# First attention: products, maxima and turned row of its first group made among the feed-forward products of the first layer

## The chip, the cores and the metric

The kernel runs on one core of a Trainium2 chip. The core has a matrix engine (TensorE, "PE" in the rows, its weight loads "PEld"), a vector engine (VectorE, "DVE"), a scalar engine (ScalarE, "ACT"), GpSimd ("POOL") and a queue that issues most transfers (SyncE, "SP" or "SPq"). They run side by side and wait for each other through semaphores. The metric is the device time of one execution in microseconds (us), lower is better; of several runs the median is given.

## The reference

Two transformer layers on x of 2 x 1024 x 256 in float32. The change lies in the first layer, where the feed-forward part and an attention of 16 heads of width 16 read the same normalised input `xn`:

```python
x = x + _L0_attn_ref(xn, ...) + _L0_ffn_ref(xn, ...)

# feed-forward: 256 -> 768 -> 256
fuse = silu(qmm(x, gate_w, gate_scale)) * qmm(x, up_w, up_scale)
return qmm(fuse, down_w, down_scale)

# attention: the plain scores, and the same with a "splat" term added
std_out = out_proj(softmax(where(mask, scores, neg)))
gsa_scores = scores + position_sensitivity * splat_attn
gsa_out = out_proj(softmax(where(mask, gsa_scores, neg)))
return (1.0 - blend) * std_out + blend * gsa_out
```

The second layer (a memory attention with sorting, a second attention, and a mixture of experts) is not touched.

## The kernel before, in words

The kernel is a list of stages. In each, every engine runs its own function (`pe`, `act`, `dve`, `pool`, `sp`), and all wait at the end of a stage until the others are there (`stage_end`). Three stages matter.

**Queries and keys** computes the records of queries and keys and stores them in the chip's main memory; its stores may go on into the next stage.

**AttentionStart together with SwiGLU** is the feed-forward part. The 2048 rows of x go in 4 blocks of 512, the 768 hidden columns in 6 slices of 128. A step is one block and one slice: 24 steps, numbered (block, slice) from (0, 0). TensorE makes in a step the four gate products `pg` and the four up products `pu`; from the second block on, slices 1 to 4 also carry the 12 down products `py` of a quarter of the block before. ScalarE makes silu (`sg`) and a rounded copy (`fh`). VectorE makes `fz` (fusing gate and up, L650), `fl` (the rest of the rounding, one step late, L656) and, in slices 2 to 5, `y` (scaling of `py`, L669). GpSimd adds `y` to x (L677). After the 24th step the down products of the last block remain. Within each engine this order is written out by hand. `pg`, `pu` and `py` have two buffers each in the accumulator memory (PSUM).
In the same stage `AttentionStart.clear` lets GpSimd wait for the stores of the records and then clear two of three places for queries and keys (L777, L778); `AttentionStart.sp` then loads groups 0 and 1 of the attention into them (16 transfers each, L761). `clear` is called by `SwiGLU.pool` after its fourth addition.

**Attention** works in 16 groups of two heads, each with plain and splat scores. A group needs, before its first score, a row that holds the negative maximum of every query. For it TensorE makes 20 units of products (`px`, L973 for the mask and L979), VectorE takes the negative maxima of each unit out of `px` (`negmax`, L1063, 20 reductions of 512 to 1024 elements on each partition), combines them (L1067, L1071), TensorE turns the result (L986), VectorE copies it (`rows`, L1078), and SyncE sends it into the queries' place (L937). `px` has two buffers. The scores (`pss`, L998) then follow, ScalarE takes the exponential (`probs`, L1035), and TensorE multiplies with the values (`po`, L1012). The order of all this is a string (`ORDERS`) in which s is a score, m a unit of maxima, v a product with values, r the row, d and t the end of a half. The m and the r of a pass through the string belong to the next group: while group g is scored, the maxima of group g + 1 are made. `schedule` puts the 20 units and the row of group 0 ahead of the first pass, since no pass precedes it.

Of the kernel before, what the change touches and what calls it, by code (L numbers as in the profile page):

```python
# [16 lines left out]
P = 128  # L17
# [553 lines left out]
class SwiGLU(Stage):  # L571
# [5 lines left out]
    SLOTS = FC + 3  # L577

    def __init__(self, k, w, start):
# [10 lines left out]
        self.gate_in, self.up_in, self.silu_made, self.fused, self.fh_made, self.fl_made, self.down_in, self.scaled, self.added = k.sems(  # L590
            "gate_in up_in silu_made fused fh_made fl_made down_in scaled added")

    def pe(self, e):
        w = self.w
        e.wait_ge(w.scales_loaded, 48)
        for i in range(NB + 1):
            x = slice(i * 512, i * 512 + 512)
            for f in range(FC):
                b, m = f % 2, i * FC + f
                if i < NB:  # L600
                    if m >= 2:
                        e.wait_ge(self.silu_made, m - 1)
                    products(e, self.pg[b][:], [(w.gw[:, c, f * P:(f + 1) * P], a[:, c, x]) for c in range(DC)
                                                for a in (self.xh, self.xl)]).then_inc(self.gate_in, 1)
                    if m >= 2:
                        e.wait_ge(self.fused, m - 1)
                    products(e, self.pu[b][:], [(w.uw[:, c, f * P:(f + 1) * P], a[:, c, x]) for c in range(DC)
                                                for a in (self.xh, self.xl)]).then_inc(self.up_in, 1)
                if i and 1 <= f <= 4:
                    n = 4 * (i - 1) + f - 1  # L610
                    e.wait_ge(self.fl_made, i * FC)
                    if n >= 2:
                        e.wait_ge(self.scaled, n - 1)
                    ts = slice((f - 1) * P, f * P)
                    products(e, self.py[n % 2][:], [(part[self.slot(i - 1, g)][:, ts], w.dw[:, g, :]) for g in range(FC)
                                                    for part in (self.fh, self.fl)]).then_inc(self.down_in, 1)

# [22 lines left out]
    def dve(self, e):  # L640
        k, w = self.k, self.w
        for m in range(NB * FC + 1):
            if m < NB * FC:
                f, b = m % FC, m % 2
                e.wait_ge(self.silu_made, m + 1)
                e.wait_ge(self.up_in, m + 1)
                if m >= 3:
# [3 lines left out]
                                       ALU.mult, ALU.mult).then_inc(self.fused, 1)  # L651
            if m:
# [18 lines left out]
    def pool(self, e):  # L671
        k = self.k
        for n in range(NT):
            if n == 4:
# [112 lines left out]

class AttentionTiles:
# [15 lines left out]
class Attention(Stage):  # L804
# [19 lines left out]
    def __init__(self, k, operands, t, records):  # L824
        self.k, self.ops, self.t, self.records = k, operands, t, records
        self.order = self.ORDERS[operands.nk]
# [96 lines left out]
    def sp(self, e):  # L923
        k, tl, t = self.k, self.ops, self.t
        for what, g, _, _ in self.units:
# [8 lines left out]
            elif what == "rows":  # L934
                e.wait_ge(self.x_read, self.places(g, "rows", None))
                rows = f32(tl.qs[g % 3][STACK:STACK + HALF + 1:HALF, :, :]).rearrange("r w (t q) -> r (w t) q", t=QT)
                e.dma_start(rows, f32(t.rows[g % 2][:])).then_inc(self.row_sent, 16)  # L937
        for p in range(3):
            e.wait_ge(self.loaded[p], 16 * tl.PARTS * len(range(p, tl.groups, 3)))
        e.wait_ge(self.row_sent, 16 * tl.groups)  # L940
# [6 lines left out]
    def pe(self, e):  # L947
        k, tl, ops = self.k, self.t, self.ops
        places, scores, maxed, std_place = 0, 0, -1, {}
        for what, g, w, arg in self.units:  # L950
# [4 lines left out]
            if what == "max":  # L955
                width, parts = arg
                diag = [t * P + P == c + width for t, c in parts][0]
# [5 lines left out]
                fresh = not ops.adds(w)  # L963
                if fresh:
# [3 lines left out]
                if diag and fresh:  # L968
                    for side in range(2):
                        for n in range(2):  # L970
                            at = HALF * n
                            to = px[:, n, 0:len(parts) * width].rearrange("p (s k) -> p s k", k=width)
                            e.matmul(to[:, :, width - P + HALF * side:width - HALF + HALF * side],  # L973
                                     k.mask_of[at:at + HALF, side, :], k.mask_by[at:at + HALF, side, 0:len(parts), :],
                                     start=side == 0, stop=False, skip_group_check=True)
                for s, (t, c) in enumerate(parts):
                    for n in range(2):
                        _, tile, at, _ = ops.of[w + n]
                        x = e.matmul(px[:, n, s * width:(s + 1) * width], ops.qs[p][at:at + STACK, tile, t * P:(t + 1) * P],  # L979
                                     ops.ks[p][at:at + STACK, tile, c:c + width], start=fresh and not diag, stop=True,  # L980
                                     skip_group_check=True)
                x.then_inc(self.x_in, 1)
            elif what == "rows":
                e.wait_ge(self.max_whole, g + 1)
                e.wait_ge(self.x_read, places - 1)
                e.matmul(px[0:4 * QT, 0, 0:P], tl.negmax[g % 2][:, 0].rearrange("p w t -> p (w t)"), k.ident[:],  # L986
                         start=True, stop=True).then_inc(self.x_in, 1)
            elif what == "scores":
# [4 lines left out]
                if scores % 48 == 0:  # L993
                    e.wait_ge(self.row_sent, 16 * (g + 1))
# [49 lines left out]
    def dve(self, e):  # L1044
        tl = self.t
        places, turns, rec, most_steps = 0, 0, Steps(self.rec_steps), Steps(self.max_steps)
        for what, g, w, arg in self.units:
# [3 lines left out]
            if what == "max":  # L1051
                width, parts = arg
                a, b = self.ops.place(w), self.ops.place(w + 1)
                of = slice(a, b + 1, b - a) if b > a else slice(a, None if b == 0 else b - 1, b - a)
                e.wait_ge(self.x_in, places)
                if len(parts) == 2:
                    out = tl.negmax[g % 2][:, :, of, parts[0][0]]
                    from_px = px[:, :, 0:2 * width].rearrange("p n (s k) -> p s n k", s=2)
                else:
                    (t, c), = parts  # L1060
# [1600 lines left out]
```

## Time and profile before

| | us |
|---|---|
| median of 3 runs | 1931.88 (1930.86 to 1935.39) |
| the profiled execution | 1928.34 |
| its span, from the first to the last instruction | 1926.6 |
| TensorE busy | 1698.7 (88%) |
| VectorE busy | 1484.1 (77%) |
| ScalarE busy | 1236.1 (64%) |
| GpSimd busy | 709.5 (37%) |

The span is what the profile sees; the time of the execution has 1.74 us around it. In the rows below all starts are in us from the start of the span. The feed-forward stage runs from 130.0 to about 203, the first attention from 203.2 on.

### The profile page before, as it was taken

The numbers are of one execution on the slowest core, as the hardware profiler recorded it, in microseconds if no ns is written. First come the engines' busy times: TensorE is split into PE (matmuls) and PEld (weight loads), VectorE is DVE, ScalarE is ACT, GpSimd is POOL, SyncE is SP. The second block draws the span as 40 slices with busy tenths as digits, with TensorE's granted clock in tenths as the row PEclk, the third lists the DMA queues.
The fourth block names the chain that finished last, engine by engine and source line by source line (L and its number), as shares of the span: only waits on it lengthen the run. The fifth ranks groups of instructions, "written<-read, shape, count | busy, mean of one in ns | idle before, by whom it ended". The sixth has DMA issues, their size and how long they took to land. (4 is left out here: it accounts for less than half of the span.)

```text
span 1926.6 us, 32116 instructions
## 1 busy us (share of the span) xinstructions
PE 1698.7 (88%) x10626; PEld 1186.8 (62%) x10626; DVE 1484.1 (77%) x3097; ACT 1236.1 (64%) x2770; POOL 709.5 (37%) x1334
## 2 busy tenths in 40 slices
PE   3989799999999888788789998887977899987998
PEld 3558444444444467576668876766865455545887
DVE  6765789999997258999997879999357698826654
ACT  2544278887778534788886678888542488865322
POOL 2003212122222215666675556666143111224632
PEclk9999599999999889888989998899988699987999
DMA  3373122333430200000000000000036333110001
GB/s 120 125 225 67 34 52 55 62 67 67 68 67 3 74 1 1 1 1 1 1 1 1 1 1 1 1 1 1 1 103 178 48 61 68 35 59 15 1 1 45
DMA packets 36132, 82.53 MB, mean 43 GB/s; under 512 B 9600, under 2 KB 11776, under 8 KB 34944
## 3 DMA queue, kind: packets, MB, share of 16 engines
q1 hardware_dynamic: 35968, 80.48, 17.2%
q8 instruction: 86, 1.41, 0.3%
q14 instruction: 78, 0.64, 0.1%
HBM read 52.79 MB, written 27.26 MB: 42 GB/s over the span
## 5 line engine op out<-in xcount | busy, mean ns | idle before, releaser
L1035 ACT ACTIVATE probs<-pss 128x512 f32<-128x512 f32 (+3 forms) x1152 | 481.7, 496 | 128.3 <-PE pss L998 127.2
L1063 DVE TENSOR_REDUCE negmax<-px 128x2 f32<-128x1024 f32 (+2 forms) x480 | 507.2, 1113 | 43.0 <-PE px L979 39.9
L1602 POOL TENSOR_SCALAR rp<-sw,tau 128x256 f32<-128x256 f32 x720 | 341.3, 507 | 7.1
L1112 POOL TENSOR_SCALAR_AFFINE_SELECT probs<-probs 128x512 f32<-128x512 f32 x192 | 120.4, 635 | 534.4 <-ACT probs L1035 534.4
L998 PE MATMUL pss<-queries,keys 64*128 64x512 f32 (+3 forms) x1152 | 295.8, 396 | 10.3 <-ACT probs L1035 5.2
L979 PE MATMUL px<-keys,queries 63*128 63x512 f32 (+3 forms) x1152 | 271.7, 429 | 13.3 <-DVE negmax L1063 13.2
L998 PEld LDWEIGHTS pss<-queries,keys 64*128 64x128 f32 x1152 | 167.4, 191 | 157.4 <-ACT probs L1035 135.7
L1012 PE MATMUL po<-probs,vals 128*32 128x512 f32 (+3 forms) x2304 | 248.8, 508 | 0.4 <-POOL probs L1112 0.2
L1451 PE MATMUL pss<-again,sw 128*128 128x256 f32 x1024 | 243.9, 397 | 0.0
L1756 DVE BATCH_NORM_STATS2 st<-rp 128x6 f32<-128x512 f32 x360 | 229.6, 674 | 2.3 <-POOL rp L1602 2.3
L1451 PEld LDWEIGHTS pss<-again,sw 128*128 128x128 f32 x1024 | 202.8, 202 | 28.5
L1436 PE MATMUL pt<-ident,sw 128*128 128x128 f32 x768 | 133.9, 306 | 83.2 <-ACT sw L1536 47.9
L1506 ACT ACTIVATE ra<-sw,neg 128x256 f32<-128x256 f32 x432 | 183.6, 525 | 4.0 <-DVE neg L1669 4.0
L979 PEld LDWEIGHTS px<-keys,queries 63*128 63x128 f32 x1152 | 133.7, 202 | 70.1 <-DVE negmax L1063 65.7
L1536 ACT ACTIVATE sw<-sw,neg 128x256 f32<-128x256 f32 x384 | 165.8, 502 | 11.8 <-DVE neg L1732 11.8
L1436 PEld LDWEIGHTS pt<-ident,sw 128*128 128x128 f32 x768 | 98.1, 155 | 120.9 <-ACT sw L1536 94.0
L1766 DVE MAX8 top<-sw 128x8 f32<-128x256 f32 x384 | 148.9, 406 | 12.6 <-ACT sw L1530 12.6
L1530 ACT ACTIVATE sw<-pss 128x1024 f32<-128x1024 f32 x96 | 97.0, 1018 | 69.1 <-PE pss L1451 48.6
L1752 DVE BATCH_NORM_STATS2 st<-ra 128x6 f32<-128x512 f32 x216 | 137.8, 671 | 3.5 <-ACT ra L1506 2.8
L1522 ACT ACTIVATE sw<-pt 128x512 f32<-128x512 f32 x192 | 108.5, 590 | 27.4 <-PE pt L1436 27.2
L1460 PE MATMUL pz<-to_out,sw 128*128 128x256 f32 x512 | 122.8, 384 | 0.0
L1451 PE MATMUL pss<-vals,xt 128*128 128x256 f32 x512 | 119.6, 394 | 1.8 <-ACT sw L1530 1.6
(366 smaller groups left out, 2645.0 us busy)
## 6 DMA issues: line engine op xcount, KB each, us to landing
queries<-rec_q SPq DMA_DIRECT2D x96, 128.0 KB, 3.6
keys<-rec_k SPq DMA_DIRECT2D x96, 128.0 KB, 3.8
queries<-rec_q SPq DMA_DIRECT2D x96, 64.0 KB, 3.5
keys<-rec_k SPq DMA_DIRECT2D x96, 64.0 KB, 3.6
rec_q<-fs SPq DMA_DIRECT2D x16, 256.0 KB, 4.1
rec_k<-fs SPq DMA_DIRECT2D x16, 256.0 KB, 4.7
rec_q<-vals SPq DMA_DIRECT2D x16, 256.0 KB
rec_k<-vals SPq DMA_DIRECT2D x16, 256.0 KB
```

What stands on the lines that cost most here:

```text
L979: x = e.matmul(px[:, n, s * width:(s + 1) * width], ops.qs[p][at:at + STACK, tile, t * P:(t + 1) * P], ops.ks[p][at:at + STACK, tile, c:c ...
L998: e.matmul(tl.pss[scores % 3][:, 512 - width:512], ops.ks[p][at:at + STACK + 1, tile, j * P:(j + 1) * P], ops.qs[p][at:at + STACK + 1, til ...
L1012: x = e.matmul(tl.po[32 * n:32 * n + 32, 512 - width:512], self.vals[:, u // H * QT + j, u % H, :], tl.probs[arg][:, n, :], start=j == 0, ...
L1035: e.activation(tl.probs[arg][:, w, :], tl.pss[scores % 3][:, 512 - width:512], ACT.Exp).then_inc(self.exp_made, 1)
L1063: e.tensor_reduce(out, from_px, X_AXIS, ALU.max, negate=True).then_inc(self.x_read, 1)
L1436: x = e.transpose(self.pt[n % 2][:, 2 * h + c, :], self.view(g, q)[:, h, c * P:(c + 1) * P], k.ident[:])
L1451: x = e.matmul(self.pss[n % 2][:, h, :], lhsT, rhs[:, 4 * half + h, c, :], start=c == 0, stop=c == 1)
L1506: x = e.activation(self.ra[n % 7][:, :, h], self.view(g, q)[:, h, :], ACT.Relu, bias=self.negated(g, r)[:, 2 * q + h:2 * q + h + 1])
L1536: x = e.activation(self.view(g, q)[:, h, :], self.view(g, q)[:, h, :], ACT.Relu, bias=self.negated(g, 3)[:, 2 * q + h:2 * q + h + 1])
L1602: x = e.tensor_scalar(self.rp[rp % 6][:, :, h], self.view(g, q)[:, h, :], -BIG, self.tau[r][:, 2 * q + h:2 * q + h + 1], ALU.min, ALU.max)
L1756: e.bn_stats(st[:, q, :], self.rp[self.bn_p % 6][:].rearrange("p n h -> p (n h)")).then_inc(self.rp_read, 1)
L1766: e.max(self.top[g % 4][:, 8 * i + h, :], self.sw[g % 5][:, i, h, :]).then_inc(self.top_made, 1)
```

## The change

The 20 units, the combination, the turn, the copy and the transfer of the row of group 0 leave the attention stage and go into the feed-forward stage, into a class of their own (`FirstMaxima`). A table `MAXIMA` says in which steps of the third and fourth block how many units are made: two in slices 1 to 4, one in slice 5 and in slice 0 of the next block. In a step with two, TensorE makes the first between `pg` and `pu`, the second at the end of the step; VectorE takes the first maximum ahead of `fz`, the second behind it. They have one `px` of their own, of two banks, so each product waits until the maximum before it has been read. The turn stands behind the down products of (4, 1), and VectorE's combining and copying between the last `fl` and the last four `y`. SyncE sends the row behind the loads. `AttentionStart.clear` is now called ahead of GpSimd's first addition. In the attention stage, `schedule` starts with the first pass for group 0, whose first score waits for the transfer of the row (`sent`).

```diff
 class SwiGLU(Stage):
     SLOTS = FC + 3
+    MAXIMA = {(2, 1): 2, (2, 2): 2, (2, 3): 2, (2, 4): 2, (2, 5): 1, (3, 0): 1, (3, 1): 2, (3, 2): 2, (3, 3): 2,
+              (3, 4): 2, (3, 5): 1, (4, 0): 1}
...
             self.py = [k.ps("py", [P, D]) for _ in range(2)]
+            first.px = k.ps("px", [P, 2, 512])
...
+                extra = iter(self.maxima(i, f))
                 if i < NB:
...
                     products(e, self.pg[b][:], ...).then_inc(self.gate_in, 1)
+                    for n in islice(extra, 1):
+                        self.first.product(e, n)
...
                     products(e, self.pu[b][:], ...).then_inc(self.up_in, 1)
                 if i and 1 <= f <= 4:
...
+                for n in extra:
+                    self.first.product(e, n)
+                if (i, f) == (NB, 1):
+                    self.first.turn(e)
...
     def dve(self, e):
+            extra = iter(self.maxima(m // FC, m % FC))
             if m < NB * FC:
+                for n in islice(extra, 1):
+                    self.first.largest(e, n)
...
                 e.scalar_tensor_tensor(self.fz[m % 3][:], ...).then_inc(self.fused, 1)
+            for n in extra:
+                self.first.largest(e, n)
             if m:
...
+        self.first.row(e)
+        self.first.copy(e)
         for n in range(4 * (NB - 1), 4 * NB):
             self.scale(e, n)
...
     def pool(self, e):
         for n in range(NT):
-            if n == 4:
+            if n == 0:
                 self.start.clear(e)
...
+class FirstMaxima:
+    def product(self, e, n):
+        if n:
+            e.wait_ge(self.x_read, n)
+        else:
+            e.wait_ge(self.ops.loaded[0], 16 * self.ops.PARTS)
+        maximum_products(e, self.k, self.ops, 0, *self.units[n], self.px).then_inc(self.x_in, 1)
+    def largest(self, e, n):
+        e.wait_ge(self.x_in, n + 1)
+        largest_of(e, self.ops, *self.units[n], self.px, self.negmax).then_inc(self.x_read, 1)
...
 class Attention(Stage):
     def schedule(self):
-        yield from self.maxima(0)
-        yield "rows", 0, None, None
+        if self.begun is None:
+            yield from self.maxima(0)
+            yield "rows", 0, None, None
...
                 if scores % 48 == 0:
-                    e.wait_ge(self.row_sent, 16 * (g + 1))
+                    if g or self.begun is None:
+                        e.wait_ge(self.row_sent, 16 * (g + 1 - self.before))
+                    else:
+                        e.wait_ge(self.begun.sent, 16)
```

`maximum_products` and `largest_of` hold what stood in `Attention.pe` and `Attention.dve` before.

VectorE in the fourth block, slices 3 and 4 (steps of the feed-forward stage). Before:

```order
L669 TENSOR_TENSOR y<-py,dsc 128x256
L650 SCALAR_TENSOR_TENSOR fz<-pu,us,sg 128x512
L656 TENSOR_TENSOR fl<-fz,fh 128x512
L669 TENSOR_TENSOR y<-py,dsc 128x256
L650 SCALAR_TENSOR_TENSOR fz<-pu,us,sg 128x512
L656 TENSOR_TENSOR fl<-fz,fh 128x512
```

Now the same two steps:

```order
L695 TENSOR_TENSOR y<-py,dsc 128x256
L848 TENSOR_REDUCE negmax<-px 128x2
L672 SCALAR_TENSOR_TENSOR fz<-pu,us,sg 128x512
L848 TENSOR_REDUCE negmax<-px 128x2
L680 TENSOR_TENSOR fl<-fz,fh 128x512
L695 TENSOR_TENSOR y<-py,dsc 128x256
L848 TENSOR_REDUCE negmax<-px 128x2
L672 SCALAR_TENSOR_TENSOR fz<-pu,us,sg 128x512
L848 TENSOR_REDUCE negmax<-px 128x2
L680 TENSOR_TENSOR fl<-fz,fh 128x512
```

Each step got two reductions, one on either side of `fz`, where there were three instructions there are five.

TensorE from the last down products of the feed-forward stage into the attention. Before, the 20 units of group 0 (`px`, L973 and L979) follow:

```order
L137 MATMUL py<-dw,fl 128x256
L973 MATMUL px<-mask_by,mask_of 128x2x64 x4
L979 MATMUL px<-keys,queries 128x128 x4
L973 MATMUL px<-mask_by,mask_of 128x2x64 x4
L979 MATMUL px<-keys,queries 128x256 x4
L979 MATMUL px<-keys,queries 128x128 x4
L979 MATMUL px<-keys,queries 128x256 x4
L973 MATMUL px<-mask_by,mask_of 128x64 x4
```

and behind their last products stand the turn, the first two units of group 1 and only then the first scores (`pss`):

```order
L973 MATMUL px<-mask_by,mask_of 128x64 x4
L979 MATMUL px<-keys,queries 128x512 x22
L986 MATMUL px<-ident,negmax 32x128
L973 MATMUL px<-mask_by,mask_of 128x2x64 x4
L979 MATMUL px<-keys,queries 128x128 x4
L973 MATMUL px<-mask_by,mask_of 128x2x64 x4
L979 MATMUL px<-keys,queries 128x256 x4
L998 MATMUL pss<-queries,keys 128x512 x2
L979 MATMUL px<-keys,queries 128x128 x4
```

Now the last down products are followed at once by group 1's first units and the scores of group 0:

```order
L137 MATMUL py<-dw,fl 128x256
L824 MATMUL px<-mask_by,mask_of 128x2x64 x4
L830 MATMUL px<-keys,queries 128x128 x4
L824 MATMUL px<-mask_by,mask_of 128x2x64 x4
L830 MATMUL px<-keys,queries 128x256 x4
L1103 MATMUL pss<-queries,keys 128x512 x2
L830 MATMUL px<-keys,queries 128x128 x4
L1103 MATMUL pss<-queries,keys 128x384
```

GpSimd ahead of and in the feed-forward stage. Before:

```order
L310 MEMSET vals 128x8192
L312 MEMSET vals 128x256
L677 TENSOR_TENSOR x<-x,y 128x256 x4
L777 MEMSET queries 128x2048
L778 MEMSET keys 128x2048
L777 MEMSET queries 128x2048
L778 MEMSET keys 128x2048
L677 TENSOR_TENSOR x<-x,y 128x256 x12
```

Now all four clearings of the places stand ahead of the sixteen additions:

```order
L310 MEMSET vals 128x8192
L312 MEMSET vals 128x256
L803 MEMSET queries 128x2048
L804 MEMSET keys 128x2048
L803 MEMSET queries 128x2048
L804 MEMSET keys 128x2048
L703 TENSOR_TENSOR x<-x,y 128x256 x16
```

## Rows read from the trace of the kernel before

**Rows 1.** Windows: us, busy and (instructions) of each engine, clock, DMA share, GB/s

```profile
205.00:210.00 5.00, 3.48 (x24) 1.95 (x22) 4.70 (x6) 0.00 (x0) 1.81 (x2) 0.50 0.00 0
...
230.00:235.00 5.00, 4.15 (x27) 3.36 (x25) 3.33 (x4) 4.92 (x10) 0.64 (x1) 0.50 0.95 181
...
240.00:245.00 5.00, 5.00 (x36) 1.77 (x36) 3.59 (x5) 2.98 (x7) 0.00 (x0) 0.79 0.00 0
```

**Rows 2.** Timeline, opening of the attention: start, us, engine, line, out<-in, [idle before <-releaser]

```profile
203.21 0.29 PE L973 MATMUL px<-mask_by,mask_of 64*128 64x128 bf16 x4 [1.39 <-POOLq L2549]
...
203.84 2.42 DVE L1063 TENSOR_REDUCE negmax<-px 128x4 f32<-128x512 f32 x3 [1.55 <-PE px L979]
...
206.56 18.56 DVE L1063 TENSOR_REDUCE negmax<-px 128x4 f32<-128x1024 f32 x17 [0.30 <-PE px L979]
...
226.62 0.60 SPq L937 DMA_DIRECT2D queries<-rows  x1
...
227.02 2.00 DVE L1063 TENSOR_REDUCE negmax<-px 128x4 f32<-128x512 f32 x2 [0.48 <-PE px L979]
...
228.69 0.80 PE L998 MATMUL pss<-queries,keys 64*128 64x512 f32 x2 [0.94 <-DMA queries<-rows]
...
229.57 1.28 ACT L1035 ACT_TABLE_LOAD   x1 [35.78 <-PE pss L998]
...
229.85 0.69 DVE L1063 TENSOR_REDUCE negmax<-px 128x4 f32<-128x512 f32 x1 [0.83 <-PE px L979]
```

**Rows 3.** Timeline, the rows' transfers of groups 1 and 2, and a maximum between

```profile
254.42 0.55 SPq L937 DMA_DIRECT2D queries<-rows  x1
...
257.62 1.82 DVE L1063 TENSOR_REDUCE negmax<-px 128x4 f32<-128x512 f32 x2 [1.46 <-PE px L979]
...
280.32 0.51 SPq L937 DMA_DIRECT2D queries<-rows  x1
```

**Rows 4.** Timeline of VectorE, feed-forward stage, one light step

```profile
159.18 0.75 DVE L650 SCALAR_TENSOR_TENSOR fz<-pu,us,sg 128x512 f32<-128x512 f32 x1
159.84 0.68 DVE L656 TENSOR_TENSOR fl<-fz,fh 128x512 fp32r<-128x512 f32 x1
160.44 0.42 DVE L669 TENSOR_TENSOR y<-py,dsc 128x256 f32<-128x256 f32 x1
160.99 0.75 DVE L650 SCALAR_TENSOR_TENSOR fz<-pu,us,sg 128x512 f32<-128x512 f32 x1
```

**Rows 5.** Timeline of TensorE, feed-forward stage, one step with down products

```profile
187.03 0.40 PE L137 MATMUL pg<-xh,gw 128*128 128x512 f32 x1
...
188.87 0.28 PE L137 MATMUL py<-dw,fh 128*128 128x256 f32 x1
...
190.28 0.40 PE L137 MATMUL pg<-xh,gw 128*128 128x512 f32 x1
```

**Rows 6.** Timeline, a unit's pair of products at full clock, first attention

```profile
250.75 0.54 PE L979 MATMUL px<-keys,queries 63*128 63x512 f32 x2
```

**Rows 7.** Timeline, end of the feed-forward stage

```profile
194.71 0.58 PE L137 MATMUL py<-dw,fh 128*128 128x256 f32 x1 [2.43 <-DVE fl L656]
...
201.87 0.43 DVE L669 TENSOR_TENSOR y<-py,dsc 128x256 f32<-128x256 f32 x1 [0.94 <-PE py L137]
```

**Rows 8.** Timeline, GpSimd's first addition and clearing, SyncE's first load

```profile
151.26 0.73 POOL L677 TENSOR_TENSOR x<-x,y 128x256 f32<-128x256 f32 x1 [136.79 <-DVE y L669]
...
161.61 1.83 POOL L777 MEMSET queries<- 128x2048 f32 x1
...
165.28 0.82 SPq L761 DMA_DIRECT2D queries<-rec_q  x2
```

**Rows 9.** Windows: the end of the stores, and of the loads of both groups

```profile
144.00:146.00 2.00, 2.00 (x11) 1.62 (x10) 1.35 (x2) 1.39 (x4) 0.00 (x0) 1.00 0.05 19
184.00:186.00 2.00, 2.00 (x12) 1.70 (x11) 0.43 (x2) 1.10 (x2) 0.73 (x1) 1.00 0.19 23
```

**Rows 10.** Windows, TensorE busy for half of a stretch, memory attention

```profile
910.00:916.00 6.00, 3.22 (x16) 2.32 (x15) 6.00 (x18) 3.92 (x8) 1.52 (x5) 1.00 0.00 0
```

More of the change, by code:

```diff
@@ L591, in __init__, with maxima @@
             "gate_in up_in silu_made fused fh_made fl_made down_in scaled added")
+    def maxima(self, i, f):
+        at = sum(c for where, c in self.MAXIMA.items() if where < (i, f))
+        return range(at, at + self.MAXIMA.get((i, f), 0))
     def pe(self, e):
@@ L785, in sp, with maximum_products @@
             t.load(self.k, e, p)
+def maximum_products(e, k, ops, g, w, arg, px):
+    width, parts = arg
+    diag = [t * P + P == c + width for t, c in parts][0]
+    fresh = not ops.adds(w)
+    if diag and fresh:
+        for side in range(2):
+            for n in range(2):
+                at = HALF * n
+                to = px[:, n, 0:len(parts) * width].rearrange("p (s k) -> p s k", k=width)
+                e.matmul(to[:, :, width - P + HALF * side:width - HALF + HALF * side],
+                         k.mask_of[at:at + HALF, side, :], k.mask_by[at:at + HALF, side, 0:len(parts), :],
+                         start=side == 0, stop=False, skip_group_check=True)
+    for s, (t, c) in enumerate(parts):
+        for n in range(2):
+            _, tile, at, _ = ops.of[w + n]
+            x = e.matmul(px[:, n, s * width:(s + 1) * width], ops.qs[g % 3][at:at + STACK, tile, t * P:(t + 1) * P],
+                         ops.ks[g % 3][at:at + STACK, tile, c:c + width], start=fresh and not diag, stop=True,
+                         skip_group_check=True)
+    return x
@@ new lines, in largest_of @@
+def largest_of(e, ops, w, arg, px, negmax):
+    width, parts = arg
+    a, b = ops.place(w), ops.place(w + 1)
+    of = slice(a, b + 1, b - a) if b > a else slice(a, None if b == 0 else b - 1, b - a)
+    if len(parts) == 2:
+        out = negmax[:, :, of, parts[0][0]]
+        from_px = px[:, :, 0:2 * width].rearrange("p n (s k) -> p s n k", s=2)
+    else:
+        (t, c), = parts
+        out = negmax[:, c // 512, of, t % 4 if c else t]
+        from_px = px[:, :, 0:width]
+    return e.tensor_reduce(out, from_px, X_AXIS, ALU.max, negate=True)
@@ L962, in pe @@
                     e.wait_ge(self.x_read, places - 2)
-                fresh = not ops.adds(w)
-                if fresh:
+                if not ops.adds(w):
                     std_place[arg] = places
@@ L967, in pe @@
                     assert places == std_place[arg] + 2
[L968 to L982, printed above, removed]
+                maximum_products(e, k, ops, g, w, arg, px).then_inc(self.x_in, 1)
             elif what == "rows":
-                e.wait_ge(self.max_whole, g + 1)
-                e.wait_ge(self.x_read, places - 1)
+                e.wait_ge(self.max_whole, g + 1 - self.before)
+                if places > 1:
+                    e.wait_ge(self.x_read, places - 1)
                 e.matmul(px[0:4 * QT, 0, 0:P], tl.negmax[g % 2][:, 0].rearrange("p w t -> p (w t)"), k.ident[:],
@@ L2485, in stages @@
             k.blend = k.sb("blend", [P, 4, 4])
+            opening = FirstMaxima(k)
             with ExitStack() as held:
```

73 lines of the change are left out of this document (47 added, 26 removed).

## The prediction

> **What bounds the kernel now.** I began with the shares of busy time in the table of the profile: TensorE 88%, VectorE 77%. As a mean they would say that TensorE is the limit everywhere. The windows say otherwise for one place. In [rows 1], first row, which stands for the opening of the attention, VectorE is busy for 4.70 of 5 us, TensorE for 3.48 at half its clock (0.50 granted, 1.2 GHz), and ScalarE for nothing. So the 20 maxima of group 0 are a stretch in which VectorE alone sets the pace and nothing else of the kernel goes on. The timeline [rows 2] gives it in order. The stage starts at 203.21, the first maximum at 203.84, the 20 reductions take 2.42 + 18.56 = 20.98 us (1.09 each on the mean; one of 1024 elements about 1.13), the row is sent at 226.62, and the first score begins at 228.69, when the transfer has landed 2.07 us later. The reader is to see that every one of these waits for the one before.
>
> The feed-forward stage is the opposite. There the timeline of TensorE [rows 5] shows a step with down products from 187.03 to 190.28, 3.25 us without a gap: 1.84 for the eight gate and up products, 1.41 for the twelve down products. A light step takes 1.81 us (159.18 to 160.99 in [rows 4]). VectorE needs per step 0.66 for `fz`, 0.60 for `fl` and 0.55 for `y`, each from start to start in [rows 4]: 1.81 in all. In a step of 3.25 it thus has 1.44 us free.
>
> **What the change removes.** The stage will begin with the same products and reductions as before, but those of group 1. Group 1's first maximum began at 227.02; it will begin where group 0's did, 0.63 us into the stage. That is 227.02 - 203.84 = 23.2 us less, for everything behind it at an unchanged pace. The scores no longer wait for the transfer: TensorE idled 0.94 us for it, and VectorE 0.83 us for the product queued behind that score [rows 2]. I add 0.8 for this. What is late next is ScalarE's table load of 1.28 us, which comes with the first exponential as before. Bounds from the nearest rows: nothing more than the 23.2, or 4.7 us more, if the first pass ran like the second. It took 27.4 us from its first maximum to the transfer of its row (227.02 to 254.42), the second 22.7 (257.62 to 280.32) [rows 2, 3]. The difference is that the first ran at half clock until about 241 ([rows 1], 0.50 and then 0.79), and had the table load. I take 24.0, with 23.2 and 27.9 as ends, since the stage still opens with light work on TensorE.
>
> **What it adds to the feed-forward stage.** First VectorE's work alone. At 160.99 it starts `fz` of step (2, 0) and is free, `fl` included, at 162.25, about when the first product can be there. From then to the last `fl` it has 11 `fz` (7.3), 12 `fl` (7.2), 8 `y` (4.4) and the 20 maxima (21.0): 39.8 us, so it ends at 202.1. Before, TensorE resumed behind the last `fl` at 194.71 [rows 7]. Without any wait the stretch is thus 7.4 us longer. This is the lower end, and it shows where the gain goes: 1.44 us free per step don't hold two maxima of 1.13.
>
> Then the waits between the two. TensorE needs little: a pair of products of 512 columns takes 0.54 from start to end [rows 6], and since such a pair overlaps, I count 0.3 of issue. But there is one `px`. In a step with two units: from the end of a second product, its maximum is read 1.25 us later (handover and 1.13), and only then the next step's first product can go; the four gate products (0.92) are over by then. After it come 0.3 + 0.92 + 1.41 + 0.3 = 2.93 for itself, up, down and the second product, and some 0.15 for the handover. The ring closes in 4.3 us, against 4.07 of VectorE's own work (1.81 + 2 x 1.13). So a step goes from 3.25 to 4.3. Eight such steps give 8.4; the first six units are narrower, and two of them, the 512-element ones, take half, which brings this to 7.4. The four steps with one unit: VectorE had no time free where there is a `y`, so (2, 5) and (3, 5) each grow by 1.13, and so does (4, 0), where the maximum stands ahead of the last `fl`; (3, 0) has no `y` and grows by 0.6. Together 4.0. The turn and the copy stand ahead of the last `y`s, and TensorE's third group of down products waits for the first of these; I give 0.3. The sum is 11.7 us. It is the same as 7.4 without waits, plus 0.2 of wait for each of 20 maxima, plus 0.3. For that wait the ends are 0 and 0.83, the longest that VectorE waited for such a product in [rows 2]: 7.7 and 24.3 us in all. I stay at 0.2, since other VectorE work stands between most products and their maxima.
>
> **What costs nothing, and what hides it.** The row's copy is over before the last four `y`, of which the last began at 201.87, and the attention stage began at 203.21 [rows 2, 7]. The transfer of 2.07 us lies beside three groups of down products and is landed when the first score asks for it. If that cover were gone, it would cost at most those 2 us. The loads must be there for the first product, at about 161.7. Stores end at about 144 (DMA share 0.05 in the first of [rows 9]). GpSimd then clears four times 1.83 us [rows 8], until 151.5. Its first addition came at 151.26 before and comes 0.3 later, without effect, since `y` has two buffers. Loads can start after two clearings, at about 148. Before, both groups took from 165.28 to about 184.5 [rows 8, 9]: 19 us, so group 0, queued first, some 9.6. It is there by 158. The margin is 4 us.
>
> **The sum.** -24.0 + 11.7 = -12.3 us. The profiled execution took 1928.34, span 1926.6 and 1.74 around it, so it would become 1916.0. That execution was 3.5 us faster than the median of the three timed runs. I apply the difference to the median: 1931.88 - 12.3 = 1919.6.
>
> **The rivals.**
> *The opening runs at the full clock.* The feed-forward stage now goes over into products and scores within about 2 us, where before 23 us at 3.5 busy of 5 held the clock at 0.50 [rows 1]. If the clock stays or comes back soon, the first pass keeps the pace of the second: 27.9 instead of 24.0, so 1915.7. Against it: the table load leaves TensorE idle right at the start.
> *The waits eat the gain.* With 0.83 us for each maximum the feed-forward stage is 24.3 longer, and nothing is left: 1932. It counts as no change from a wait of about 0.5 on, where the gain falls under 5.8. For it speaks the single `px`; against it that up and down products (2.33) stand between the units of a step, and `fl` and `y` between its last and the next.
> *The loads are late.* If group 0 is there only with group 1 (20 us after 148), the first product waits 6 us, in front of all later gate products: 1925.6. The rate in [rows 9] speaks against it.
> *The clock falls in the feed-forward stage.* This is the case that ends slower. TensorE will now idle in every busy step, 4.3 less 3.85 of work, and if its clock went to 1.2 GHz, a step would be bound by TensorE at twice 3.85 = 7.7: 4.4 more for each of eight, some 2.3 for each of four, about 44 us in place of 11.7. The time would be 1952. It decides from about half of the stretch on, since 24 us are won. Against it: in [rows 10] TensorE is busy for only 3.22 of 6 us and the granted clock is 1.00, while here it would be near 90%.
> The Trainium skill (TensorE: Matmul & The Clock Gate, Part 1, "What's actually happening") says that "the default state is throttled, and activity releases the throttle". By that rule alone more idle time is a danger in the feed-forward stage, and denser work a help in the opening; the trace agrees with the second in its 0.50 of the thin opening, and its row of half-busy time at 1.00 says that the small gaps of the first don't suffice.
>
> **How the numbers follow.** Chances: the forecast 0.60, its own range 1916 to 1923.5; full clock in the opening 0.20; waits that eat the gain 0.10; late loads 0.05; the fallen clock 0.05. A measurement of this kernel tells about 0.3% (5.8 us) from no change. Below 1926 lie the forecast, the full clock, the late loads at their price and part of the waits: 0.88. Within 0.3% lies most of the waits: 0.07. Slower 0.05. The range from 1913 to 1926 takes in the opening's upper end with a small extension of the other stage, and waits up to 0.5; outside it are the fallen clock and the larger waits.
>
> **What would show it.** In the profile after: the first `pss` about 1.5 us behind the stage's first `px`, not 25.5. The stage's start at about 215 instead of 203.2. Steps of the fourth block at 4.3 us with VectorE busy near 95% and TensorE idle for some 0.4 behind `negmax`. The granted clock 1.00 until the last `fl`. SyncE's loads from about 148 on, and no wait of the first `px` for them. The forecast is wrong if the steps are far from 4.3, if the attention's first row transfer of a group comes later than 28 us after the stage's start, or if the later groups, 25.9 us apart (254.42 to 280.32 [rows 3]), change their pace.

## The result, and the profile after

| | before | after |
|---|---|---|
| median of 5 runs | 1932.23 us (1930.86 to 1937.46) | 1923.63 us (1919.46 to 1925.35) |
| ratio, 95% interval | | 0.995 (0.9932 to 0.9968) |
| profiled execution, span | 1928.34, 1926.6 | 1919.46, 1917.7 |

The change made the kernel 8.6 us faster by the medians, 8.9 by the profiled executions; 12.3 were forecast. (The kernel before has five runs here, and had three, with a median of 1931.88, in the table ahead of the prediction.) To find the difference I cut both traces at five places: the first gate product of the feed-forward stage (130.00 before, 130.83 after), `fz` of step (2, 0), `fz` of step (3, 5), the start of the next stage (GpSimd's clearing), and the transfer of group 1's row. The `fz` of (2, 0) and group 1's row of the kernel before stand in [rows 4] and [rows 3] (160.99 and 254.42), the changed kernel's row below. Of the other marks, first of the kernel before and then of the changed one:

```profile
192.38 0.75 DVE L650 SCALAR_TENSOR_TENSOR fz<-pu,us,sg 128x512 f32<-128x512 f32 x1
203.26 1.80 POOL L1103 MEMSET queries<- 128x2048 f32 x1 [0.17 <-POOLq L2549]
```
```profile
162.82 0.75 DVE L672 SCALAR_TENSOR_TENSOR fz<-pu,us,sg 128x512 f32<-128x512 f32 x1
207.64 0.74 DVE L672 SCALAR_TENSOR_TENSOR fz<-pu,us,sg 128x512 f32<-128x512 f32 x1
220.25 1.81 POOL L1198 MEMSET queries<- 128x2048 f32 x1 [0.17 <-POOLq L2646]
```

| stretch | before | after | change | forecast |
|---|---|---|---|---|
| a: first `pg` to `fz` of (2, 0) | 30.99 | 31.99 | +1.0 | 0 |
| b: to `fz` of (3, 5), the steps with units | 31.39 | 44.82 | +13.4 | 11.7 |
| c: to the start of the attention stage | 10.88 | 12.61 | +1.7 | (in b) |
| d: to the transfer of group 1's row | 51.16 | 26.25 | -24.9 | -24.0 |

Outside these, the stage began 0.8 later and the rest of the kernel took 1.0 less. Nothing ties these or a to the change: over the eleven later traces a ranges from 31.08 to 32.64, and the first `pg` from 129.75 to 134.78, and of one kernel (experiment 6) a was 31.1 and 32.4. The kernel before has only one trace. What moved with the change is b, c and d: 15.2 given back, 24.9 won.

The opening first. The timeline after, as [rows 2 and 3]:

```profile
220.20 0.29 PE L824 MATMUL px<-mask_by,mask_of 64*128 64x128 bf16 x4 [1.39 <-POOLq L2646]
...
220.82 3.65 DVE L848 TENSOR_REDUCE negmax<-px 128x4 f32<-128x512 f32 x4 [1.54 <-PE px L830]
220.97 0.39 PE L1103 MATMUL pss<-queries,keys 64*128 64x512 f32 x2
221.44 1.28 ACT L1140 ACT_TABLE_LOAD   x1 [12.39 <-PE pss L1103]
...
246.50 0.55 SPq L1053 DMA_DIRECT2D queries<-rows  x1
...
272.41 0.51 SPq L1053 DMA_DIRECT2D queries<-rows  x1
```

The first maximum comes 0.62 us into the stage, as before, but it is group 1's, and the first score 0.77 us into it, where it took 25.5. The first pass takes 25.7 us from its first maximum to its row (27.4 before), and the next row follows 25.9 later as before. The windows, as [rows 1], have the likely reason why the pass is still slower than a later one (22.7 from its first maximum to its row in the kernel before):

```profile
220.00:225.00 5.00, 3.92 (x40) 2.46 (x40) 3.88 (x5) 3.55 (x6) 3.63 (x3) 0.96 0.04 14
225.00:230.00 5.00, 4.88 (x33) 3.88 (x32) 4.55 (x5) 3.92 (x13) 1.85 (x3) 0.50 0.77 185
230.00:235.00 5.00, 5.00 (x22) 2.24 (x20) 2.81 (x4) 2.59 (x7) 0.64 (x1) 0.52 0.57 121
235.00:240.00 5.00, 5.00 (x42) 2.22 (x41) 4.97 (x5) 4.33 (x10) 0.00 (x0) 1.00 0.00 0
```

The granted clock is 0.96 in the first 5 us, about 0.50 (1.2 GHz) in the next ten, and 1.00 (2.4 GHz) after them.

Now the price. VectorE's timeline for a step with two units, (3, 3), beside [rows 4]:

```profile
196.65 0.42 DVE L695 TENSOR_TENSOR y<-py,dsc 128x256 f32<-128x256 f32 x1
196.98 1.22 DVE L848 TENSOR_REDUCE negmax<-px 128x2 f32<-128x1024 f32 x1
198.11 0.74 DVE L672 SCALAR_TENSOR_TENSOR fz<-pu,us,sg 128x512 f32<-128x512 f32 x1
199.70 1.23 DVE L848 TENSOR_REDUCE negmax<-px 128x2 f32<-128x1024 f32 x1 [0.84 <-PE px L830]
200.84 0.68 DVE L680 TENSOR_TENSOR fl<-fz,fh 128x512 fp32r<-128x512 f32 x1
201.44 0.42 DVE L695 TENSOR_TENSOR y<-py,dsc 128x256 f32<-128x256 f32 x1
```

It takes 4.79 us (196.65 to 201.44), not 4.3, and VectorE waits 0.84 of it for the second product. The four busy steps of the fourth block take 4.47 to 4.99. TensorE's timeline of the same time, as [rows 5 and 6]:

```profile
194.16 0.28 PE L137 MATMUL py<-dw,fl 128*128 128x256 f32 x1
194.37 0.50 PE L830 MATMUL px<-keys,queries 63*128 63x512 f32 x2
194.80 0.50 PE L137 MATMUL pg<-xh,gw 128*128 128x512 f32 x1
195.14 0.39 PE L137 MATMUL pg<-xl,gw 128*128 128x512 f32 x1
...
196.19 0.51 PE L830 MATMUL px<-keys,queries 63*128 63x512 f32 x2 [0.20 <-DVE negmax L848]
196.62 0.50 PE L137 MATMUL pu<-xh,uw 128*128 128x512 f32 x1
```

Read the starts, not the durations. From the pair's start to that of the next `pg` are 0.43; from this `pg` to the second 0.34, where 0.23 is usual; and the pair itself starts 0.21 behind the last `py`, where 0.12 is usual. The pair costs 0.43 + 0.11 + 0.09 = 0.63 us, and around this pair the profile shows no idle time of TensorE. I had counted 0.3. Finally the end of the stage, as [rows 7]:

```profile
209.23 1.22 DVE L848 TENSOR_REDUCE negmax<-px 128x2 f32<-128x1024 f32 x1
210.36 0.68 DVE L680 TENSOR_TENSOR fl<-fz,fh 128x512 fp32r<-128x512 f32 x1
...
211.10 0.58 PE L137 MATMUL py<-dw,fh 128*128 128x256 f32 x1 [2.82 <-DVE fl L680]
...
214.87 0.60 SPq L900 DMA_DIRECT2D queries<-rows  x1
```

The last maximum stands ahead of the last `fl`, as forecast. The row is sent at 214.87 and had landed when the first score asked at 220.97.

### The profile page after: what moved, and what is told of

It reads as the page before. It is cut to its first block and busy times, and to the rows that moved or that the text cites. A ratio compares the mean times of both kernels' runs of the same rounds, so it can differ in the third digit from the quotient of the medians.

```text
span 1917.7 us, 32118 instructions
## 1 busy us (share of the span) xinstructions
PE 1695.6 (88%) x10626; PEld 1182.1 (62%) x10626; DVE 1482.4 (77%) x3097; ACT 1236.2 (64%) x2770; POOL 709.7 (37%) x1334
## 5 line engine op out<-in xcount | busy, mean ns | idle before, releaser
L830 PE MATMUL px<-keys,queries 63*128 63x512 f32 (+3 forms) x1152 | 265.6, 418 | 10.5 <-DVE negmax L848 10.5
L830 PEld LDWEIGHTS px<-keys,queries 63*128 63x128 f32 x1152 | 130.3, 196 | 64.9 <-DVE negmax L848 61.7
```

The costliest lines, as they stand in the source:

```text
L830: x = e.matmul(px[:, n, s * width:(s + 1) * width], ops.qs[g % 3][at:at + STACK, tile, t * P:(t + 1) * P], ops.ks[g % 3][at:at + STACK, ti ...
```

## The experiments

In all of them the table's stretches are given, since the time of a kernel moves by several us with stages that no edit touches (single runs of the kernel before: 1924.7 to 1941.7). In the thirteen traces the first attention from group 1's row to group 14's took 336.7 to 336.9 us, so nothing in it takes a gain back; all that follows took 1332.7 to 1341.9. In this last part the traces of the changed kernel and of experiments 3 and 7 have at most 1334.8, the five of experiments 5, 6 and 8 with spaced units 1337.5 to 1341.6, but those of experiments 1, 2 and 4 have 1337.8 to 1341.9 as well, and the kernel before 1335.4. Why is open, so a gain of one to four us in the stretches below is not shown to be one of the whole kernel.

**1. Clearing late again.** The part of the change on GpSimd is undone.

```diff
-            if n == 0:
+            if n == 4:
                 self.start.clear(e)
```

> The changed kernel with one part undone: GpSimd clears the places after its fourth addition again, as before, and not ahead of the first. Theory (the early clearing is what lets the maxima begin in the third block): the loads start at about 167 us instead of 149, group 0 has landed near 176, and the first unit of products waits for it on TensorE some 12 us behind the gate products of step (2, 1), with nothing to do meanwhile; the feed-forward stage ends 12 us later (about 232 in the trace), the time goes from 1923.6 to about 1935, so above the kernel before. Rival (the clearing could have stayed where it was, the loads are quick enough): no wait, 1923 to 1925.

Measured: 1939.9 us, ratio to before 1.0036 (1.0017 to 1.0056), where 1935 was expected. Stretch b is 61.7, c 13.9. TensorE's timeline has the wait; the first load was issued at 167.26:

```profile
178.52 0.39 PE L824 MATMUL px<-mask_by,mask_of 64*128 64x128 bf16 x4 [14.71 <-DMA keys<-rec_k]
```

The early clearing is a condition of the change; without it the kernel is slower than before. The wait was 14.7 us and not 12, since group 0 lands 11.3 us after its first issue; the prediction took 9.6. The granted clock was 0.50 from 170 to 178.5, in the wait, and still so from 178.5 to 181, and b grew by 16.8, which is 2.1 more than the wait. In the changed kernel (first issue 149.33) group 0 lands near 160.6 by the same 11.3, an estimate, 3 us before the first product at 163.56.

**2. The early clearing alone**, in the kernel before, as the counterpart.

```diff
-            if n == 4:
+            if n == 0:
                 self.start.clear(e)
```

> The kernel before with only the early clearing (ahead of GpSimd's first addition), the maxima left in the opening of the attention. Theory (it is a condition, not a gain): the loads move from 165 to about 149, nobody waits for them, the feed-forward stage and the opening are as before: the next stage begins at 203 to 204 and the first score 25.5 us later, 1928 to 1933. Rival (the earlier loads or the late first addition disturb the stage, and the 1.8 us by which the changed kernel's third block began later are its price): the third block begins near 162.8 as in the changed kernel, and the time is 1 to 2 us longer than before.

Measured: 1939.5 us (one run), where 1928 to 1933 were expected. The feed-forward stage's late start of 134.78 is 4.8 of the difference, a 1.7, b to d together 0.9, and 3.8 lie behind group 1's row. b 31.5, c 11.2, d 51.7, within about 0.5 of the kernel before each, so the clearing alone does nothing to the stretches that moved with the change. a was 32.6, which is what the rival foresaw, but in two traces with the early clearing (the first of the tail kernel below, and the repeated changed one) it was 31.1, and in experiment 1, without it, 31.4; so the clearing isn't what makes it long.

**3. Thin maxima.** VectorE reads only 16 columns of each part (`cut` is 16 for group 0), so the maxima are not those of the whole rows.

```diff
+    if cut:
+        from_px = from_px[:, :, :, 0:cut] if len(parts) == 2 else from_px[:, :, 0:cut]
     return e.tensor_reduce(out, from_px, X_AXIS, ALU.max, negate=True)
```

> The changed kernel with VectorE's 20 reductions of group 0 cut to the first 16 columns of each part (the maxima are then not the maxima of the whole rows); TensorE's products are as they were. What is left is TensorE's price of the units. Theory (each change between the feed-forward's 128-row products and the 63-row pairs holds TensorE up, about 0.63 us for a unit where the prediction counted 0.3): steps with two units in the fourth block take 3.25 + 2 x 0.63 = 4.5 us instead of the 4.75 of the changed kernel, and the feed-forward stage is only about 2 us shorter. Rival (VectorE's own work is the limit, as the prediction had it): the steps fall to 3.9 or less, and the stage is 6 to 8 us shorter.

Measured (one run, 1915.5 us): b 43.3, the busy steps of the fourth block 4.46 to 4.52 us, against 4.47 to 4.99 before the cut. With VectorE's reductions down from 1.13 to as little as 0.1 us from start to start, 1.5 us of the 13.4 went away. The limit in b is TensorE: (43.3 - 31.4) / 19 = 0.63 us for each of the 19 units in it. The prediction's view of this stretch, VectorE first, is refuted. c fell too, from 12.6 to 10.3, so the two are 3.8 us shorter, where the theory had 2 and the rival 6 to 8. Of c, 1.0 is the maximum ahead of the last `fl` (`fz` of (3, 5) to the first of the last down products: 2.4 us instead of 3.5); the other 1.3 go with the granted clock, which was 1.00 from 207 to 217 and 0.89 and 0.77 in the changed kernel. TensorE's matmuls and weight loads in b:

```profile
193.35 0.50 PE L830 MATMUL px<-keys,queries 63*128 63x512 f32 x2
193.78 0.50 PE L137 MATMUL pg<-xh,gw 128*128 128x512 f32 x1
194.12 0.39 PE L137 MATMUL pg<-xl,gw 128*128 128x512 f32 x1
```
```profile
193.35 0.19 PEld L830 LDWEIGHTS px<-keys,queries 63*128 63x128 f32 x2
193.78 0.19 PEld L137 LDWEIGHTS pg<-xh,gw 128*128 128x128 f32 x1 [0.24 <-issue]
```

The weights of the first `pg` behind the pair are loaded from 193.78 on, with the matmul, and not ahead of it.

**4. The same with products over all 128 rows.**

```diff
+            of = slice(0, P) if whole else slice(at, at + STACK)
-            x = e.matmul(..., ops.qs[g % 3][at:at + STACK, tile, t * P:(t + 1) * P],
+            x = e.matmul(..., ops.qs[g % 3][of, tile, t * P:(t + 1) * P],
...
```

The same goes for the keys (`ops.ks`), and `whole` is set for the 20 units alone. The products mix two heads, so the numbers are others.

> As the one with thin reductions, and each of the 40 products of the 20 units uses all 128 rows of the places in place of 63 (it mixes the two heads, so the numbers are others), so that the two of a pair no longer run beside each other, but have the form of the feed-forward products around them. Theory (the change of form costs): a pair then takes 2 x 0.23 = 0.46 us with no loss around it, a step with two units 3.25 + 0.92 = 4.2 us, less than the 4.5 of the thin kernel although the array has twice the work. Rival (the 0.63 is the pair's own time, or that of the semaphores): a unit costs 0.23 more than in the thin kernel, and a step 4.9 us.

Measured (one run, 1922.2 us): b 42.0, the busy steps of the fourth block 4.15 to 4.19. Twice the rows take less time there. In the third block, where some units also have mask products of 64 rows (L824) and the busy steps' parts are narrower, these steps are as in the thin kernel (4.26 to 4.56, against 4.41 to 4.48). The single runs say nothing here: 7.2 us more of this one lie behind group 1's row. The rows:

```profile
193.47 0.63 PE L831 MATMUL px<-keys,queries 128*128 128x512 f32 x2
193.93 0.39 PE L137 MATMUL pg<-xh,gw 128*128 128x512 f32 x1
194.16 0.40 PE L137 MATMUL pg<-xl,gw 128*128 128x512 f32 x1
```
```profile
193.70 0.19 PEld L137 LDWEIGHTS pg<-xh,gw 128*128 128x128 f32 x1
193.93 0.19 PEld L137 LDWEIGHTS pg<-xl,gw 128*128 128x128 f32 x1
```

The pair takes 0.46 from start to start, twice 0.23 with nothing around it, and the weights of `pg` come 0.23 ahead of it. A step is 3.25 + 2 x 0.46 = 4.17. So 0.63 is not the price of the work, which is twice as much here, nor that of the semaphores, which are the same: what is left is the change between 128-row and 63-row products and back. The Trainium skill has the rule (TensorEngine Tiling (Array Packing), Key Properties): a change of the tiling mode drains TensorE. These runs agree. If two overlapping halves need 0.23, half of the 0.46 (an estimate; no run has such a pair by itself), the two changes around a pair cost 0.63 - 0.23 = 0.4 us. The prediction did not weigh this rule.

**5. Spaced units.** TensorE makes the first unit of a step behind the up products, VectorE takes the maxima behind `fz` and behind `fl`.

```diff
-                    for n in islice(extra, 1):
-                        self.first.product(e, n)
                     if m >= 2:
                         e.wait_ge(self.fused, m - 1)
                     products(e, self.pu[b][:], ...).then_inc(self.up_in, 1)
+                    for n in islice(extra, 1):
+                        self.first.product(e, n)
```

VectorE's part of the edit is not printed.

> The changed kernel with the first unit of a step moved behind the up products (it stood between gate and up), and VectorE's order fz, first maximum, fl, second maximum, y. The two units of a step are then 1.4 and 1.8 us of other products apart, in place of 2.3 and 0.9. Theory (a ring over the one px adds the wait behind the gate products, 4.75 - 4.5 = 0.25 us a step, and TensorE's 4.5 stay): steps of 4.5 us, the stage some 2 to 3 us shorter, 1921 us. In the light steps the maximum no longer stands ahead of fz, and in (4, 0) it stands behind the last fl, which gives 1 us of this. Rival (VectorE is the limit with 4.07 and its waits for products): nothing in the steps, at most the 1 us of (4, 0).

Measured: 1920.9 us, ratio 0.9937 (0.9923 to 0.9952), which overlaps that of the changed kernel. b 43.3 instead of 44.8, the busy steps of the fourth block 4.54 to 4.57 (one 4.79). Of the 1.5 us, 0.7 are the two steps that had taken 4.99 and 4.80, and 0.7 the first step, where the maximum now stands behind `fz`; the other busy steps stayed within 0.14. In the steps the wait for `px` behind the gate products is gone, and VectorE's waits for a product are too (0.4 us in all, 7.5 in the changed kernel). TensorE's 4.5 remains. VectorE's work is unchanged, so the rival falls, but the 2 to 3 us expected of the stage were 1.4. c stayed 12.7: the 1 us of (4, 0) did not show, since the maximum of (3, 5) now stands behind its `fz`, and so it is this one that the last `fl` waits for (3.46 us from `fz` of (3, 5) to the first of the last down products in both kernels).

**6. Units in the tail.** Spaced, and two more units behind the down products of (4, 1) and (4, 2), out of (3, 3) and (3, 4). The turn goes behind those of (4, 3).

```diff
-              (3, 0): 1, (3, 1): 2, (3, 2): 2, (3, 3): 2,
-              (3, 4): 2, (3, 5): 1, (4, 0): 1}
+              (3, 0): 1, (3, 1): 2, (3, 2): 2, (3, 3): 1,
+              (3, 4): 1, (3, 5): 1, (4, 0): 1, (4, 1): 1, (4, 2): 1}
...
-        self.first.row(e)
-        self.first.copy(e)
-        for n in range(4 * (NB - 1), 4 * NB):
+        for n in range(2):
+            self.first.largest(e, 18 + n)
+            if n:
+                self.first.row(e)
+            self.scale(e, 4 * (NB - 1) + n)
+        self.first.copy(e)
+        for n in range(4 * NB - 2, 4 * NB):
             self.scale(e, n)
```

> The spaced kernel (units behind the up products), and two units more taken out of the busy steps (3, 3) and (3, 4) and put behind the first two groups of down products of (4, 1) and (4, 2), where VectorE has only the scalings to do; the row is combined there and turned after the third group. Theory: each unit out of a busy step saves its 0.63 us of TensorE, in the tail it fills waits for the last fl and is nearly free, 1.0 to 1.5 us less than spaced, about 1919.5. The transfer of the row lands within 0 to 1 us of the next stage's first score. Rival (the transfer is now late): the first score waits for the row, and the gain is lost: 1921 or more.

> Spaced units and the tail, once more. Its trace gave 2.9 us less than the spaced kernel and 4.3 less than the changed one from the start of the feed-forward stage to group 1's row, its time did not show it (1923.3). Theory (the time before was noise of other stages): ratio 0.992 to 0.994, below that of the changed kernel. Rival (something later takes the gain back): 0.995 as the changed kernel.

Measured: 1923.3, ratio 0.9951 (0.9933 to 0.9969), and again 1921.1, 0.9950 (0.9931 to 0.9969). The steps with one unit take 3.88 = 3.25 + 0.63, b is 41.7 in both, 1.6 less than spaced. c is 12.9 with two more units in it, and 14.2 the second time, when the granted clock from 207 to 212 was 0.66 (1.00 the first time). The transfer left at 214.56 in the first trace, 3.5 us ahead of the first score, so it is not late. In the stretches b + c this is 1.5 and 0.1 less than spaced. The 0.992 to 0.994 expected of the repetition did not come, and the times don't show a gain over the changed kernel; whether one is there stays open.

**7. Early table load.** The changed kernel with one exponential at the end of ScalarE's part of the feed-forward stage.

```diff
+        e.activation(self.sg[0][:, 0:1], self.sg[0][:, 0:1], ACT.Exp)
```

> The changed kernel with one small exponential on ScalarE at the end of the feed-forward stage, so that the table load of 1.28 us is done there, under the last down products. This is for the opening of the attention. Theory (the first pass takes 25.7 us from its first maximum to its row instead of 22.7 because TensorE idles behind the table load and the clock then falls to 0.50 for about 7 us): the load gone, the clock either stays at 1.00 and the first pass takes 23 to 24 us, 1.5 to 3 us less in all, or the clock falls nevertheless and only about 1 us is won. Rival (VectorE sets the pace of the pass from the start): nothing.

Measured: 1921.6, ratio 0.9944 (0.9924 to 0.9964). ScalarE's timeline, and the windows:

```profile
207.86 1.28 ACT L658 ACT_TABLE_LOAD   x1
209.16 0.20 ACT L658 ACTIVATE sg<-sg 128x1 f32<-128x1 f32 x1
220.27 1.47 ACT L1141 ACTIVATE probs<-pss 128x512 f32<-128x512 f32 x3 [10.91 <-PE pss L1104]
```
```profile
220.00:225.00 5.00, 4.16 (x33) 2.81 (x31) 4.97 (x6) 3.96 (x9) 3.24 (x3) 0.81 0.21 54
225.00:230.00 5.00, 5.00 (x31) 3.61 (x34) 4.54 (x6) 3.62 (x12) 1.85 (x3) 0.50 0.65 172
```

The load is under the down products, and d is 25.8 where the changed kernel has 26.3 and, repeated, 27.0. The clock fell all the same, so the table load is not what brings the clock down, and of the expectation's cases the second is left, at 0.5 to 1.2 us. But that is no more than d moves by itself: the other traces without the early load have 25.6 (experiment 1) to 26.9. Beside the tail kernel, 25.7 twice, the kernel with both has 25.4 twice. So a gain of 0.3 us is likely, and more is not shown.

**8. All three together**, that is the edits of experiments 5, 6 and 7 in one kernel, and the changed kernel repeated, without an edit, on the same chip as the second run of all three.

> Spaced units, the two units in the tail and the early table load together. If the three are independent, the sum of their gains: 2.7 of the spacing, 1 to 1.5 of the tail, 1 to 3 of the table load, so 1916 to 1919, and faster than both the kernel before and the changed one. If the clock or the row's transfer takes one of them back, about 1920.

> Spaced units, tail and early table load, once more. Theory: as the tail version and about 0.5 us less, 0.992 to 0.994. Rival: 0.995 as the changed kernel.

> The changed kernel once more, beside the two best versions on one chip, because the median of one kernel moves by several us between groups of runs. Expected: the ratio of its first measurement, 0.995 (0.993 to 0.997). In its trace the feed-forward stage from the third block on (first fz of block 3 to the next stage) takes 57.4 us again, whatever the stages before it do.

| | median | ratio to before, 95% | b | c | d |
|---|---|---|---|---|---|
| all three | 1919.7 | 0.9928 (0.9902 to 0.9954) | 41.8 | 14.3 | 25.4 |
| all three, repeated | 1918.1 | 0.9933 (0.9908 to 0.9958) | 41.7 | 12.8 | 25.4 |
| changed kernel, repeated | 1922.9 | 0.9962 (0.9945 to 0.9979) | 44.8 | 13.7 | 27.0 |

With all three, b + c + d is 81.5 and 79.9, against 83.7 and 85.5 of the changed kernel: 4 us less on the mean, but the part behind the first attention was longer in the traces (see above). The medians of the repeated pair, beside each other on one chip, differ by 4.9. The intervals against the kernel before still overlap a little, so the version is shown faster than before, and likely, but not by the times alone, faster than the changed kernel. The repeated changed kernel gave 58.5 for b + c where 57.4 were expected: b was the same to 0.01, c longer, with a granted clock of 0.59 and 0.73 from 212 to 222.

## Why the prediction was right, and where it was off

The direction held, and so did the exchange: the opening's stretch goes, and a smaller price is paid in the feed-forward stage. 1923.6 lies in the range of 1913 to 1926, 0.1 beyond the end of the likeliest case's own (1923.5). What sets that price was wrong: the prediction put VectorE's own work first, and it is TensorE's, with the ring over the one `px` on top. The number came out as near as it did partly by luck: the price was 3.5 us higher than forecast, and the opening gave 0.9 more. By the prediction's steps:

- *What is removed: 24.0.* It was 24.9. The 23.2 of shift are exact (0.63 us to the first maximum before, 0.62 after), and the added 0.8 for the faster pass were 1.7. The rival of the full clock did not come about: the clock held for 5 us and then fell for ten.
- *What is added: 11.7.* It was 15.2. The step that failed is "I count 0.3 of issue" for a pair of products. A pair took 0.63, with the change from 128-row to 63-row products and back in it (experiments 3 and 4). The estimate came from the duration of a pair in the attention, not from starts. The kernel before had rows with a hint. A pair ahead of a score of 64 rows has 0.33 from its start to the next, already more than 0.3, and one ahead of a product of 128 rows (`po`) has 0.43, as between the feed-forward products:

```profile
248.49 0.50 PE L979 MATMUL px<-keys,queries 63*128 63x512 f32 x2 [0.41 <-DVE negmax L1063]
248.82 0.40 PE L998 MATMUL pss<-queries,keys 64*128 64x512 f32 x2
...
268.55 0.50 PE L979 MATMUL px<-keys,queries 63*128 63x512 f32 x2
268.98 0.85 PE L1012 MATMUL po<-probs,vals 128*32 128x384 f32 x8
```

- *The order of the limits.* The prediction had VectorE ahead (4.07 a step) and TensorE's own work at 3.85. With 0.63 a unit, TensorE has 4.51 and is ahead of it, and thin maxima gave back only 1.5 us. The ring over the one `px` exists as described, with its parts longer: it closes at 4.8 instead of 4.3. Spacing the units took 0.45 and 0.23 off two of the eight steps and little off the others (experiment 5). The waits of VectorE for a product were 7.5 us in all, 0.37 for each maximum against the 0.2 forecast:

```profile
DVE negmax L848 <- PE px L830: 7.5, 9, 1.0
```

  Put into the prediction's second sum they give 7.4 + 7.5 + 0.3 = 15.2, the measured price. That is no proof of it: in experiment 5 these waits fell to 0.4 and b + c by only 1.4.

- *The tail: 0.3, and 1.1 for the maximum of (4, 0).* Measured c + 1.7. From `fz` of (3, 5) to the first of the last down products it is 1.1 more (3.46 against 2.33), from there to the next stage 0.6 more.
- *The loads.* In time, with a margin of about 3 us, not 4. That the move of the clearing carries the change was right, and weighs more than thought: 16 us.
- *The clock in the feed-forward stage.* It stayed at 1.00, as the prediction said, in spite of the waits:

```profile
175.00:205.00 30.00, 29.41 (x164) 20.97 (x164) 24.74 (x33) 8.68 (x14) 3.70 (x5) 1.00 0.01 2
```

- *The signs.* The first score came 0.8 us into the stage, sooner than the 1.5 named, and the later groups kept their 25.9. The next stage began at 220.2 and not at 215, VectorE was busy for 82% from 175 to 205 (24.74 of 30) and not for 95, and TensorE idled 0.20 behind `negmax` and not 0.4: this is how it looks when TensorE is ahead.
- *A reading.* The 20 reductions took 20.98 / 20 = 1.05 us each on the mean, not 1.09; the sum used 21.0 for all and is not touched by it.

Outside the terms, 0.8 us of a later start and 1.0 of a longer stretch a entered the profiled result, and 1.0 less at the other end. a's length goes with the granted clock at the beginning of the stage: from 130 to 135 it was 0.72 in the kernel before and 0.50 in the changed one, and from 135 to 140 1.00 and 0.92.

## What to carry to other kernels

Work that only one engine does while the others stand still is worth moving under a stage where that engine is half free, even if it doesn't fit in for nothing: here the 20 maxima with their row took 24.9 us of the opening, 1.25 each, and gave back 15.2 in the other stage, 0.76 each. Price a TensorE instruction by its neighbours and from start to start: a pair of products of another row count set between full ones cost 0.63 us, more than the 0.46 of a pair with twice the work in their own form. No run here gathers such pairs; to make two of them side by side would be the next thing to try. A match of the sum is not a proof of the limit: take the supposed limit away, as experiment 3 did, and see. Before trusting such a move, find out what it needs early: without the earlier clearing and loads, the same change is a loss.

## What the runs showed of the hardware

A pair of 63-row products between 128-row ones holds TensorE for 0.63 us, a pair of 128-row products in the same place for 0.46. The weight load that follows is not taken ahead after a 63-row pair (it starts with its matmul, at 193.78 in experiment 3), and is taken 0.23 us ahead after a 128-row pair (193.70 for a matmul at 193.93 in experiment 4). TensorE's busy time hides this: the profile has it busy for 29.41 of 30 us from 175 to 205 in the changed kernel.

TensorE's granted clock was 1.00 ahead of a wait of 14.7 us in which it did nothing, 0.50 from 170 on in it and for the first 2.5 us behind it, and 1.00 again from 184 on (experiment 1).
